# Two gated attention layers with mixtures of experts on one core: the first layer's experts computed for the chosen tokens only

## The chip, the cores and the metric

The kernel runs on one core of a Trainium2 chip, in float32 except where it splits numbers into bfloat16 parts. The metric is the device time of one execution in microseconds (us), the median of several. One execution of each kernel is also recorded by the hardware profiler. Engine names are those of the profile: PE is TensorE's matmuls, PEld its weight loads, DVE VectorE, ACT ScalarE, POOL GpSimd, SP SyncE, which issues most DMAs.

## The reference, cut to what matters

The input x is 16 batches of 256 tokens of width 256. Four units follow one another, each added to x with a gate tanh(g): unit 0, cross attention of 16 heads; unit 1, self attention plus a mixture of 8 linear experts; unit 2, attention over context and tokens; unit 3, causal attention, a second, larger mixture of experts, and norms. Unit 1 is what the change is about:

```python
    def _L0_ffn_ref(x, W_qkv, b_qkv, W_gate, b_gate, W_experts, b_experts):   # E = 8, TOP_K = 2, D = 256
        ...
        attn_out = jnp.einsum('bhqk,bkhd->bqhd', attn, v).reshape(B, S, D)
        gate = jax.nn.softmax(x @ W_gate + b_gate, axis=-1)
        top_g, top_i = jax.lax.top_k(gate, TOP_K)
        combine = jnp.sum(jax.nn.one_hot(top_i, E, dtype=x.dtype) * top_g[..., None], axis=2)
        expert_out = jnp.einsum('bsd,edf->bsef', x, W_experts) + b_experts
        moe_out = jnp.einsum('bsef,bse->bsf', expert_out, combine)
        return attn_out + moe_out
    ...
    x = x + jnp.tanh(g_xattn[0]) * _L0_xattn_ref(ctx_2048, _layernorm(x, axis=-1), L0_xattn_b, itok_Bx1_68_817)
    x = x + jnp.tanh(g_ffn[0]) * _L0_ffn_ref(_layernorm(x, axis=-1), L0_ffn_W_qkv, ...)
```

## The kernel before, in words

The kernel has two phases. The attention phase does all four units. Its work is cut into 64 jobs (u, b), a unit and a batch, unit by unit, and each job into steps: XT transposes the normalised rows; K, Q, V are projections; KSPLIT and QSPLIT (POOL, three operations each) split them into bfloat16 parts, which go through memory (STACK, ROWS) to become operands; S are scores whose row maxima DVE takes; M (POOL, five small operations) and MT bring the maxima in place; T are the scores again, of which ACT takes the exponentials; PV is the product with the values; OT turns the result back, and FIN adds it to x. Each token tile has 128 rows, so a batch has two.

Which engine does which step when is not left to the hardware. A planner (`orders`) plays the steps at build time with a cost per step (`STAGES`) and writes down one fixed order for each engine (`ORDER`), looking at most eight jobs ahead. Each engine then works down its list and waits on semaphores. A step that waits holds up all that stands behind it on its engine. Small rings of buffers tie jobs to each other: the transposed rows `xt` have three buffers, so XT of a job waits until the third job before it has used its own; `o` has three, `xs` seven, and the steps in `PRE` (XT, K, Q, V and all that makes expert results) share two PSUM banks.

In unit 1 each job also has the mixture. GATE computes logits, GEXP and six TOP steps (DVE) the two best experts and a weight for all eight, with zeros for six. MBIAS starts the sum with the weighted biases, and 8 EXPERT steps per job (two experts each, both halves of the inner dimension) compute all eight experts for all tokens, of which DVE adds each with its weight:

```python
                    elif name == "EXPERT":
                        t, e = k
                        end_pre(step, pe.matmul(bank[:, :], xt_now[:, turn, t * P:(t + 1) * P], wexp[:, turn, e:e + 2, :].rearrange("p e n -> p (e n)"),
                                                start=turn == 0, stop=ends), ends)
```

The second phase, the expert phase, does unit 3's large mixture in another way: `route` sorts all tokens by expert into 71 slot tiles of 128 rows (64 full ones and one more for each of seven experts), and `run_experts` fetches the rows of a tile with an indirect DMA, computes one expert for them, and stores the results with another. `combine` adds them. This phase is not touched.

## Time and profile before

| | us |
|---|---|
| median of three runs | 2621.05 (2614.16 to 2621.49) |
| the profiled execution, its own time | 2617.61 |
| its span, first to last instruction | 2615.9 |
| unit 0, to its last FIN | 361.6 |
| unit 1, from there to its last FIN | 617 |
| unit 2, from there to 1566 | 587 |
| unit 3, to 1902 | 336 |
| sorting, expert phase and combine | 714 |

Times below are read on the profiled execution, from the start of its span. The stage borders are starts of the last step of a unit; the stages overlap by some tens of us, as the first steps of a unit begin during the one before it.

### The profile page before, as it was taken

Reading aid. Unit: us, or ns where it says so; the run is one execution under the profiler, and the core shown is the slowest. Engines: PE = TensorE matmul, PEld = TensorE weight load, DVE = VectorE, ACT = ScalarE, POOL = GpSimd, SP = SyncE. Lnnn points to the kernel's source line nnn. Section 1 sums busy time; section 2 is a strip of 40 time slices with the busy share of each in tenths; the row PEclk is TensorE's granted clock in tenths of the full one; section 3 lists DMA queues with packets and bytes.
Section 4 is the critical chain, followed back from the end, with each engine's and each line's share of the span. In section 5 each row is a group of like instructions: output and inputs, shape, how many; then the busy total and the mean of one; then the engine's idle time right before and its main releaser. Section 6 shows DMA issues by size and latency. Waiting matters only on the chain. (4 is left out here: it accounts for less than half of the span.)

```text
span 2615.9 us, 52259 instructions
## 1 busy us (share of the span) xinstructions
PE 2282.1 (87%) x17492; PEld 1575.9 (60%) x17493; DVE 1686.8 (64%) x4481; ACT 1362.3 (52%) x2398; POOL 978.5 (37%) x1850
## 2 busy tenths in 40 slices
PE   2889999899999999999999999899848999999910
PEld 1445555555455556666666666666538999999910
DVE  4878886676767666777767668767563444443458
ACT  3889863454336346777777777767601222222211
POOL 5555412213122225333322247878602333333321
PEclk7999998999899999999999999999958999999965
DMA  7878623315134245544455445555180111111144
GB/s 216 206 192 208 148 67 82 88 38 122 30 88 95 65 99 135 116 116 113 112 118 120 107 116 109 122 133 129 42 277 27 34 36 37 36 36 32 35 173 156
DMA packets 209839, 275.49 MB, mean 105 GB/s; under 512 B 32606, under 2 KB 156489, under 8 KB 203370
## 3 DMA queue, kind: packets, MB, share of 16 engines
q1 hardware_dynamic: 196074, 242.38, 37.3%
q0 software_dynamic: 6912, 17.97, 2.2%
q10 hardware_dynamic: 6656, 12.58, 1.3%
q8 instruction: 116, 1.90, 0.3%
q14 instruction: 81, 0.66, 0.1%
HBM read 193.12 MB, written 80.64 MB: 105 GB/s over the span
## 5 line engine op out<-in xcount | busy, mean ns | idle before, releaser
L1035 ACT ACTIVATE ex<-t_ps 128x512 f32<-128x512 f32 (+1 forms) x1280 | 685.7, 579 | 203.0 <-PE t_ps L941 157.9
L1183 DVE TENSOR_REDUCE mx<-s_ps 128x2 f32<-128x512 f32 (+1 forms) x1024 | 659.9, 683 | 197.2 <-PE s_ps L912 125.2
L941 PE MATMUL t_ps<-qs,ks 123*128 123x256 bf16 x2048 | 355.5, 277 | 8.7 <-ACT ex L1035 3.7
L964 PE MATMUL pv_ps<-ex,va 128*17 128x256 f32 (+1 forms) x5120 | 318.1, 374 | 1.3 <-POOL ex L1087 1.3
L1029 ACT ACTIVATE qs<-tr_ps 27x2048 bf16<-27x2048 bf16 x128 | 239.2, 1869 | 108.3 <-PE tr_ps L925 105.5
L882 PE MATMUL pre_ps<-wexp,xt 128*128 128x512 f32 x512 | 270.5, 634 | 3.1 <-DVE moe L1242 2.2
L941 PEld LDWEIGHTS t_ps<-qs,ks 123*128 123x128 bf16 x2048 | 176.9, 98 | 156.1 <-ACT ex L1035 68.2
L1582 PEld LDWEIGHTS x_up_ps<-x_rows_t,x_wnow 128*128 128x128 f32 x2272 | 266.4, 193 | 5.3 <-issue 0.9
L1582 PE MATMUL x_up_ps<-x_rows_t,x_wnow 128*128 128x128 f32 x2272 | 267.0, 276 | 1.1 <-DVE x_pre L1645 0.7
L1592 PE MATMUL x_y_ps<-wdn,x_act 128*128 x1136 | 257.1, 379 | 0.7 <-DVE x_y L1653 0.7
L1612 ACT ACTIVATE x_rows_t<-x_rt_ps 128x256 f32<-128x256 f32 x72 | 27.6, 383 | 436.7 <-PE x_rt_ps L1571 436.7
L1592 PEld LDWEIGHTS x_y_ps<-wdn,x_act 128*128 128x128 f32 x1136 | 210.3, 190 | 26.8 <-issue 1.1
L1095 POOL TENSOR_SCALAR mp<-mx 128x16 bf16<-128x16 f32 x128 | 34.3, 268 | 512.2 <-DVE mx L1183 492.9
L918 PE MATMUL s_ps<-ks,qs 99*128 99x256 bf16 (+1 forms) x1024 | 186.6, 284 | 36.2 <-DVE mx L1183 24.7
L964 PEld LDWEIGHTS pv_ps<-ex,va 128*17 128x17 f32 x5120 | 124.8, 97 | 139.3 <-issue 49.9
L1176 DVE CUSTOM_DVE_ANT_0 s_ps<-s_ps,late 128x128 f32<-128x128 f32 (+1 forms) x512 | 166.8, 388 | 45.4 <-PE s_ps L915 45.2
L912 PE MATMUL s_ps<-ks,qs 96*128 96x256 bf16 x1024 | 180.0, 274 | 15.0 <-DVE mx L1183 8.5
L1640 DVE COPY x_wnow<-wup 128x1024 f32 x144 | 98.9, 688 | 144.9 <-issue 82.9
L1242 DVE SCALAR_TENSOR_TENSOR moe<-pre_ps,comb,moe 128x256 f32<-128x256 f32 x256 | 123.4, 482 | 91.2 <-PE pre_ps L882 84.3
L1039 ACT ACTIVATE ot<-pv_ps 128x256 f32<-128x256 f32 x256 | 99.8, 390 | 133.2 <-PE pv_ps L964 130.8
L918 PEld LDWEIGHTS s_ps<-ks,qs 99*128 99x128 bf16 (+1 forms) x1024 | 86.4, 100 | 126.6 <-DVE mx L1183 73.3
L1078 POOL TENSOR_TENSOR ak<-ak,pk 128x512 f32<-128x512 f32 x64 | 74.7, 1167 | 218.8 <-ACT pk L1016 112.5
(248 smaller groups left out, 3739.7 us busy)
## 6 DMA issues: line engine op xcount, KB each, us to landing
q_parts<-pq SPq DMA_DIRECT2D x128, 192.0 KB
qs<-q_parts SPq DMA_DIRECT2D x64, 384.0 KB, 4.9
qs<-q_parts SPq DMA_DIRECT2D x192, 128.0 KB, 5.8
k_parts<-pk SPq DMA_DIRECT2D x96, 192.0 KB
ks<-k_parts SPq DMA_DIRECT2D x96, 192.0 KB
ks<-k_parts SPq DMA_DIRECT2D x288, 64.0 KB
ks<-ctx_k_parts SPq DMA_DIRECT2D x64, 192.0 KB
ks<-ctx_k_parts SPq DMA_DIRECT2D x192, 64.0 KB
```

The lines of the kernel that those rows point to most:

```text
L882: end_pre(step, pe.matmul(bank[:, :], xt_now[:, turn, t * P:(t + 1) * P], wexp[:, turn, e:e + 2, :].rearrange("p e n -> p (e n)"), start=t ...
L912: last = pe.matmul(dst[:, r * T:(r + 1) * T], q(src), key(r)[0:rows, h, :], start=True, stop=True)
L918: last = pe.matmul(dst[:, t * T:(t + 1) * T], q(t), key(0)[0:rows, h, :], start=True, stop=True)
L941: last = pe.matmul(dst[:, t * T:(t + 1) * T], key[0:ROWS, h, t * P:(t + 1) * P], qs[q_at][0:ROWS, h, :], start=True, stop=True)
L964: last = pe.matmul(pv_ps[i * VS:i * VS + VW, q0:T], val[:, t, k * QH + i, :], e, start=r == 0 and t == 0, stop=r == srcs - 1 and t == NT - ...
L1029: act.activation(qs[q_at][PRODUCTS:ROWS, k * HG:(k + 1) * HG, :], tr_b[PRODUCTS:ROWS, 0:T].unsqueeze(1).broadcast_to([ROWS - PRODUCTS, HG, ...
L1035: act.activation(ex[:, n % EXPS, 0:w], t_ps[n % 2][:, 0:w], ACT.Exp).then_inc(t_read, 1)
L1176: last = dve.tensor_tensor_reduce(out=seen, in0=seen, in1=late[:, 2 * P - w:2 * P], scale=1.0, scalar=FUTURE, op0=ALU.add, op1=ALU.max, ac ...
L1183: dve.tensor_reduce(dst, s_ps[n % S_BANKS][:, :].rearrange("p (a b) -> p a b", a=dst.shape[-1]), AX.X, ALU.max).then_inc(s_read, 1)
L1242: last = dve.scalar_tensor_tensor(out=moe[r][:, t, :], in0=bank[:, n * D:(n + 1) * D], scalar=comb[r][:, t, e + n:e + n + 1], in1=moe[r][: ...
L1582: last = pe.matmul(up_ps[h][:, g * P:(g + 1) * P], wnow[k][h][:, c, g * P:(g + 1) * P], rows_t[:, c, :], start=c == 0, stop=c == DC - 1)
L1592: last = pe.matmul(y_ps[:, 0:D], act_t[k][h][:, g, :], wdn[:, bass.ds(x, 1), f, :].rearrange("p e n -> p (e n)"), start=f == 0, stop=f == ...
```

## The change

The mixture of unit 1 is taken out of its jobs and done by slots, as the expert phase does the larger one.

- Unit 0 gains, after FIN of each batch: HNS, HNP, HNX (moments and normalised rows of the new x, DVE and POOL), STOREN (the rows to memory, SP), HT (transposed, PE and ACT) and HG (the gate's logits, PE and DVE). Unit 1 loads the rows (LOADN) and no longer computes them. HT writes the `xt` buffer of its job, and XT of unit 1 waits until HG of three jobs before has read it.
- When all 16 batches have their logits, a chain of 23 RC steps on DVE (some 75 instructions, each of which waits for the one before it), with RX, RANK and NAME on ACT, PE and POOL, sorts the tokens into 71 tiles. It is the computation of `route`, and it runs beside the first jobs of unit 1.
- Each of the 71 tiles has XR (POOL: indirect DMA of 128 rows into one of six buffers), XTT (PE fetches the number of the tile's expert into a register, then two transposes; ACT copies), XE (PE: the bias as a product of a one-hot with the three bfloat16 parts of the biases, then two products of 256 columns; DVE copies to one of four buffers) and XS (POOL: indirect DMA to memory). The planner counts them to jobs 2 to 7 of unit 1.
- GATE, GEXP, TOP, CT, MBIAS, EXPERT and FIN's addition of the mixture are gone. Unit 2 gains LOADY (512 KB of expert rows) and MOE (DVE, four additions) per job, ahead of its moments.
- Unit 3's weights `w1` and `wo` move into the memory of the spent experts and are loaded in unit 2. In the first block of the program the biases are loaded three times behind the expert weights, and DVE makes their parts, before it turns `w1x`.

```diff
+HOTS = 4
+NER, NY = 6, 4
+CHAIN = 23
+def tile_job(n):
+    return 1, 2 + n // 12
...
-    "GATE": [("pe", 0.9), ("dve", 0.65)], "GEXP": [("act", 0.22)], "TOP": [("dve", 0.6)],
-    "CT": [("pe", 0.25), ("act", 0.36)], "MBIAS": [("pe", 1.1), ("dve", 0.69)], "EXPERT": [("pe", 0.87), ("pe", 0.87), ("dve", 0.97)],
+    "XR": [("pool", 1.25), ("wire", 4.5)], "XTT": [("pe", 0.55), ("act", 0.39)], "XE": [("pe", 1.0), ("dve", 0.42)], "XS": [("pool", 1.25), ("wire", 4.5)],
...
-    free = [past(n, NQ, 0, (1, 2, 3)) for n in ("K", "Q", "V")] + [past("EXPERT", NQ, (t, e), (1,)) for t in range(NT) for e in range(0, E, 2)]
+    free = [past(n, NQ, 0, (1, 2, 3)) for n in ("K", "Q", "V")] + [past("HG", NQ, 0, (0,))]
...
+    for n in range(SLOT_TILES):
+        add(of("XR", n), rc(CHAIN - 1), of("XTT", n - NER))
+        add(of("XTT", n), of("XR", n), of("XE", n - 2))
+        add(of("XE", n), of("XTT", n), of("XS", n - NY))
+        add(of("XS", n), of("XE", n))
...
-                sp.dma_start(bexp[:, :], a["b0_exp"]).then_inc(small_loaded, 16)
...
-                sp.dma_start(w1[:, :, :], chunked(a["w1_qkv"])).then_inc(w_loaded, 16)
-                sp.dma_start(wo[:, :, :], chunked(a["w1_o"])).then_inc(w_loaded, 16)
+                for n in range(3):
+                    sp.dma_start(bexp[n * E:(n + 1) * E, :], a["b0_exp"]).then_inc(small_loaded, 16)
...
+                    elif name == "XTT":
+                        if k == 0:
+                            pe.wait_ge(tables_ready, 1)
+                        chosen[k] = pe.value_load(expert_of[0:1, k:k + 1], min_val=0, max_val=E - 1)
+                        begin_pre(step)
+                        pe.wait_ge(er_loaded[k % NER], 16 * (k // NER + 1))
+                        for c in range(DC):
+                            last = pe.transpose(bank[:, c * P:(c + 1) * P], er[k % NER][:, c * P:(c + 1) * P], ident[:, :])
                         end_pre(step, last)
-                    elif name == "EXPERT":
-                        t, e = k
-                        end_pre(step, pe.matmul(bank[:, :], xt_now[:, turn, t * P:(t + 1) * P], wexp[:, turn, e:e + 2, :].rearrange("p e n -> p (e n)"),
-                                                start=turn == 0, stop=ends), ends)
+                    elif name == "XE":
+                        wait_copied(pe, ("XTT", u, b, k))
+                        x = chosen.pop(k)
+                        pe.matmul(bank[:, 0:D], tile_is[:, k:k + 1].broadcast_to([3 * E, P]), bexp_parts[:, :], start=True, stop=False)
+                        for c in range(DC):
+                            last = pe.matmul(bank[:, 0:D], ert[k % 2][:, c, :], wexp[:, c, bass.ds(x, 1), :].rearrange("p e n -> p (e n)"),
+                                             start=False, stop=c == DC - 1)
+                        end_pre(step, last)
...
+                    elif name == "XR":
+                        if k == 0:
+                            pool.wait_ge(tables_ready, 1)
...
+                        if k >= NER:
+                            wait_turned(pool, ("XTT", *tile_job(k - NER), k - NER))
+                        pool.indirect_dma_start(er[k % NER], None, n1_d.rearrange("b p t n -> (b p t) n"),
+                                                bass.IndirectOffsetOnAxis(ap=row_of[:, k:k + 1].bitcast(U32), axis=0)).then_inc(er_loaded[k % NER], 16)
+                    elif name == "XS":
+                        wait_copied(pool, ("XE", u, b, k))
+                        pool.indirect_dma_start(y1_d.rearrange("b p t n -> (b p t) n"), bass.IndirectOffsetOnAxis(ap=dest_of[:, k:k + 1], axis=0),
+                                                ey[k % NY], None, bounds_check=ROWS_OUT - 1, oob_is_err=False).then_inc(y_stored[k % NY], 16)
...
+                    elif name == "MOE":
                         dve.wait_ge(x_loaded[x_at], 16 * (nth_x + 1))
+                        dve.wait_ge(y_loaded[b % 2], 16 * (b // 2 + 1))
+                        for m in range(TOPK):
+                            for t in range(NT):
+                                last = dve.scalar_tensor_tensor(out=xs[x_at][:, t, :], in0=yb[b % 2][:, t * TOPK + m, :], scalar=first_share[:, b * NT + t, m:m + 1],
+                                                                in1=xs[x_at][:, t, :], op0=ALU.mult, op1=ALU.add)
```

How the change moves instructions, at three places. The first is PE where the first projection of unit 1 stands (`pre_ps<-xt,w`). `s_ps` are scores, `t_ps` the scores again; 16 heads of a batch make 32 matmuls of each. Before:

```order
L821 MATMUL pre_ps<-ident,xn 128x128 x4
L918 MATMUL s_ps<-ks,qs 128x256 x2
L975 MATMUL tr_ps<-ident,ot 128x128 x2
L918 MATMUL s_ps<-ks,qs 128x256 x2
L941 MATMUL t_ps<-qs,ks 128x256 x2
L918 MATMUL s_ps<-ks,qs 128x256 x2
L941 MATMUL t_ps<-qs,ks 128x256 x2
L975 MATMUL tr_ps<-ident,ot 128x128 x2
L964 MATMUL pv_ps<-ex,va 17x256 x8
L941 MATMUL t_ps<-qs,ks 128x256 x4
L925 MATMUL tr_ps<-ident_b,mp 27x128 x2
L918 MATMUL s_ps<-ks,qs 128x256 x4
L826 MATMUL pre_ps<-xt,w 128x256 x2
```

After; `ident,o` is HT, `wg,xt` is HG and `ident,xn` is XT of the first job of unit 1:

```order
L968 MATMUL pre_ps<-ident,o 128x128 x4
L1091 MATMUL tr_ps<-ident_b,mp 27x128 x2
L1130 MATMUL pv_ps<-ex,va 17x256 x8
L980 MATMUL pre_ps<-wg,xt 128x8 x4
L1084 MATMUL s_ps<-ks,qs 128x256 x4
L968 MATMUL pre_ps<-ident,xn 128x128 x4
L1107 MATMUL t_ps<-qs,ks 128x256 x4
L1141 MATMUL tr_ps<-ident,ot 128x128 x2
L1084 MATMUL s_ps<-ks,qs 128x256 x4
L973 MATMUL pre_ps<-xt,w 128x256 x2
```

Before, 384 of unit 0's 512 `t_ps` matmuls stand ahead of this projection; now 468 do, with 56 of the 64 matmuls of HG.

The second place is PE in the middle of the expert tiles. Before, between attention steps, one EXPERT turn (`pre_ps<-wexp,xt`) at a time:

```order
L918 MATMUL s_ps<-ks,qs 128x256 x4
L941 MATMUL t_ps<-qs,ks 128x256 x2
L882 MATMUL pre_ps<-wexp,xt 128x512
L941 MATMUL t_ps<-qs,ks 128x256 x4
L918 MATMUL s_ps<-ks,qs 128x256 x4
L882 MATMUL pre_ps<-wexp,xt 128x512
L941 MATMUL t_ps<-qs,ks 128x256 x4
L964 MATMUL pv_ps<-ex,va 17x256 x8
```

After (`ident,work` are the transposes of XTT, the ISA rows handle the register):

```order
L1043 MATMUL pre_ps<-bexp_parts,tile_is 128x256
L1045 ISA
L1045 MATMUL pre_ps<-wexp,work 128x256
L1045 ISA
L1045 MATMUL pre_ps<-wexp,work 128x256
L1043 MATMUL pre_ps<-bexp_parts,tile_is 128x256
L1045 ISA
L1045 MATMUL pre_ps<-wexp,work 128x256
L1045 ISA
L1045 MATMUL pre_ps<-wexp,work 128x256
L1034 TENSOR_LOAD first_expert_of
L1034 ISA x2
L1038 MATMUL pre_ps<-ident,work 128x128 x2
L1107 MATMUL t_ps<-qs,ks 128x256 x2
```

From the first fetch of an expert's number to the last expert product PE has 71 tiles and 178 `t_ps` matmuls, the attention of 5.6 jobs; 78 matmuls (2.4 jobs) of unit 1 stand ahead of it, and 8 jobs behind it.

The third place is POOL in the same stretch (`work<-normed` is XR, `first_expert_rows<-work` is XS, `ak`, `pk` are KSPLIT, `aq`, `pq` QSPLIT):

```order
L1237 DMA first_expert_rows<-work,first_dest_of 8192x256
L1233 DMA work<-normed,first_row_of 128x256 x3
L1262 TENSOR_TENSOR ak<-ak,pk 128x512
L1264 CAST pk<-ak 128x2x256
L1266 TENSOR_TENSOR pk<-ak,pk 128x2x256
L1262 TENSOR_TENSOR aq<-aq,pq 128x512
L1264 CAST pq<-aq 128x2x256
L1266 TENSOR_TENSOR pq<-aq,pq 128x2x256
L1237 DMA first_expert_rows<-work,first_dest_of 8192x256 x4
L1233 DMA work<-normed,first_row_of 128x256 x4
L1237 DMA first_expert_rows<-work,first_dest_of 8192x256 x2
L1233 DMA work<-normed,first_row_of 128x256 x2
```

Before, POOL had in unit 1 only such splits, the five operations of M and two for the moments of a job. Now 142 indirect DMAs stand there, with 12 M and 8 splits between the first and the last of them.

## Rows read from the trace of the kernel before

**Rows 1.** The page: busy time, share of the span and instructions of each engine.

```profile
PE 2282.1 (87%) x17492; PEld 1575.9 (60%) x17493; DVE 1686.8 (64%) x4481; ACT 1362.3 (52%) x2398; POOL 978.5 (37%) x1850
```

**Rows 2.** Windows by stage: length, busy time (instructions) of PE PEld DVE ACT POOL, PEclk, DMA share, GB/s.

```profile
31.00:361.60 330.60, 281.61 (x2495) 157.71 (x2496) 256.88 (x578) 258.81 (x439) 174.61 (x329) 0.94 0.75 180
361.60:978.70 617.10, 578.35 (x3333) 318.62 (x3332) 424.31 (x1040) 281.07 (x512) 143.94 (x282) 0.95 0.31 76
978.70:1566.00 587.30, 567.72 (x5142) 368.09 (x5140) 414.34 (x899) 441.40 (x757) 200.44 (x370) 0.99 0.50 116
1902.00:1971.00 69.00, 30.14 (x133) 28.74 (x133) 43.47 (x108) 0.42 (x1) 1.16 (x6) 0.50 0.81 259
```

**Rows 3.** FIN: its source line up to 362.4, and in the whole trace.

```profile
L1263 DVE SCALAR_TENSOR_TENSOR xs<-o,tanh_g,xs x16: 751/752/1427, 97.1 to 361.6; 128x512 f32<-128x512 f32 x16
...
L1263 DVE SCALAR_TENSOR_TENSOR xs<-o,tanh_g,xs x32: 750/752/1530, 97.1 to 978.7; 128x512 f32<-128x512 f32 x32
```

**Rows 4.** Groups of the whole trace: what the change removes.

```profile
L882 PE MATMUL pre_ps<-wexp,xt 128*128 128x512 f32 x512 | 270.5, 634 | 3.1 <-DVE moe L1242 2.2 <-DVE va L1167 0.8
...
L1242 DVE SCALAR_TENSOR_TENSOR moe<-pre_ps,comb,moe 128x256 f32<-128x256 f32 x256 | 123.4, 482 | 91.2 <-PE pre_ps L882 84.3
...
L878 PE MATMUL pre_ps<-bexp,combt 8*128 8x256 f32 x64 | 20.8, 450 | 10.8 <-DVE va L1167 10.3 <-DVE moe L1242 0.5
```

**Rows 5.** Windows of 5 us in unit 1, columns as in rows 2.

```profile
420.00:425.00 5.00, 0.90 (x5) 0.23 (x3) 4.90 (x11) 0.57 (x2) 4.64 (x6) 0.90 0.92 223
425.00:430.00 5.00, 4.86 (x14) 3.51 (x15) 2.28 (x10) 0.22 (x1) 1.65 (x3) 0.50 0.92 186
430.00:435.00 5.00, 5.00 (x8) 1.81 (x6) 2.06 (x11) 0.00 (x0) 0.00 (x0) 0.57 0.58 170
```

**Rows 6.** Timeline of the first block: start, us, engine, line, [idle before].

```profile
7.11 1.09 SPq L592 DMA_DIRECT2D wexp<-in_L_ffn_W_experts  x2
...
13.72 0.17 DVE L655 TENSOR_SCALAR bqk<-bqk 128x2 f32<-128x2 f32 x1
...
22.87 0.85 DVE L662 COPY wproj<-s_ps 128x256 f32<-128x256 f32 x2 [0.36 <-PE s_ps L683]
```

**Rows 7.** Window of 150 us within unit 0, columns as in rows 2.

```profile
150.00:300.00 150.00, 136.67 (x1288) 75.58 (x1290) 124.15 (x270) 131.64 (x222) 78.89 (x156) 0.99 0.79 185
```

**Rows 8.** Groups of the whole trace: nearest to what is added.

```profile
L826 PE MATMUL pre_ps<-xt,w 128*128 128x256 f32 x512 | 130.0, 383 | 2.8 <-ACT xt L998 1.7 <-DVE moe L1242 0.9
...
L1571 PE MATMUL x_rt_ps<-ident,x_rows 128*128 128x128 f32 x144 | 27.9, 275 | 8.4 <-DMA x_rows<-h_normed,x_row_now 8.4
...
L1149 DVE BATCH_NORM_STATS2 hstats<-o 128x6 f32<-128x256 f32 x32 | 12.0, 418 | 0.5
...
L1159 DVE TENSOR_SCALAR o<-o,hmv,hrstd 128x256 f32<-128x256 f32 x32 | 14.0, 479 | 1.9 <-POOL hrstd L1059 1.9
```

**Rows 9.** Groups of the whole trace: POOL's indirect DMAs and one part of a split.

```profile
L1535 POOL DMA_INDIRECT x_rows<-h_normed,x_row_now x73 | 73.1, 1001 | 62.3 <-POOL x_row_now L1533 58.9 <-DVE x_y L1653 3.5
...
L1543 POOL DMA_INDIRECT expert_rows<-x_y,x_dest_now x71 | 79.9, 1125 | 65.4 <-POOL x_dest_now L1541 65.4
...
L1078 POOL TENSOR_TENSOR ak<-ak,pk 128x512 f32<-128x512 f32 x64 | 74.7, 1167 | 218.8 <-ACT pk L1016 112.5 <-ACT pk L1014 91.7 <-ACT pk L1006 14.6
```

**Rows 10.** Timeline in the expert phase.

```profile
2210.13 1.25 POOL L1543 DMA_INDIRECT expert_rows<-x_y,x_dest_now  x1 [0.92 <-POOL x_dest_now L1541]
2210.56 0.69 DVE L1640 COPY x_wnow<-wup 128x1024 f32 x1 [1.78 <-PE x_up_ps L1582]
...
2217.38 1.00 POOL L1543 DMA_INDIRECT expert_rows<-x_y,x_dest_now  x1 [0.92 <-POOL x_dest_now L1541]
2218.33 0.69 DVE L1640 COPY x_wnow<-wup 128x1024 f32 x1 [2.31 <-issue]
```

**Rows 11.** Source line of PE's fetch in the expert phase: ns min/median/max.

```profile
L1564 PEldq TENSOR_LOAD <-expert_of x71: 298/312/498, 1980.8 to 2488.1; - x71
```

**Rows 12.** Source line L1535, the gathers of the expert phase, from issue to landing.

```profile
DMA to landing us min/median/max: 2.7/2.8/4.1
```

476 lines of the change are left out of this document (345 added, 131 removed).

## The prediction

> **What bounds the kernel now.** I began with the page's totals: PE is busy for 87% of the span [rows 1], but that is a mean over stages, so the windows by stage came next [rows 2]. They say which engine sets the pace of each. In unit 1, where the change works, PE is busy 578 of 617 us (94%), DVE 69%, ACT 46%, POOL 23%, the DMA engines 31%: a stage bound by PE. Unit 2 is so still more (568 of 587 us). Unit 0 is another matter. FIN of its 16 batches starts between 97.1 and 361.6 [rows 3], a pitch of 17.6 us, and a window in its middle shows PE at 91%, ACT 88%, DVE 83% and DMA 79% [rows 7]: four resources close together.
>
> The costliest groups then say what PE's time in unit 1 is: the dense experts are 270.5 us of PE and the weighted additions 123.4 us of DVE [rows 4]. Their sizes, 512 records in 256 matmuls of 512 columns, make 1.06 us a matmul. Last, windows of 5 us show how the stage runs: at 420 PE stands for 4 us while DVE and POOL are full, and the next 10 us have a granted clock of 0.50 and 0.57, the lower level (1.2 GHz) or mostly so [rows 5]: 4 us idle and 5 lost to the clock. The clock of the whole stage is 0.95 [rows 2], 31 us of 617 at most, which six such stalls would explain.
>
> **The change, step by step.** The profiled execution took 2617.6 us for a span of 2615.9, 3.4 us under the median of the runs; the sum is made on it. First the pieces that are added or removed in unit 1.
>
> - PE, removed: 270.5 + 20.8 (MBIAS) [rows 4], and 16 pairs of small transposes at 0.39 [rows 8], 6: 297 us.
> - PE, added: a 256-column float32 matmul costs 130.0 us over 256 (512 records), 0.51 us; the two transposes of a tile 27.9 over 72, 0.39 us [rows 8]. The one-hot product (24 rows, bfloat16) is in no row; it lies between nothing and a float32 one of the same width, 0.51; I take 0.25. A tile is 0.39 + 2 x 0.51 + 0.25 = 1.66 us, 71 tiles 118 us. NAME adds at most the 30 us of PE in the sorting stage, at a clock of 0.50 [rows 2]; 15 at full clock.
> - DVE, removed 123 us and the TOP steps; added 71 copies of some 0.4 us, and the chain, priced by the sorting stage that does the same: 43.5 us busy [rows 2].
> - POOL, added: 71 gathers of 1.00 us and 71 stores of 1.13, 151 us [rows 9].
>
> What is left to an attention job of unit 1? About 5% of its expert matmuls start ahead of the stage's border, so I give the window 95% of the unit, 15.1 jobs. PE: the mixture is 297 us, and GATE with 64 products of 8 columns at most 18 at the 0.28 of the smallest matmuls in rows 8; 95% of 315 is 299, and 578 - 299 = 279 us are 18.5 a job. ACT: 281 over 15.1, 18.6 us [rows 2]. So once the experts are away a job has two engines at 18.6 us, and by unit 0's ratio (a pitch of 17.6 with a busiest engine of 0.91 x 17.6 = 16.1 [rows 3, 7]) its pitch is 20.3.
>
> Now the terms.
>
> *First block, +6.* DVE now passes its wait for the small loads at once (13.72), and ends its last copy at 23.7 [rows 6]. The new loads stand behind 2 MB of experts issued at 7.1; at the 180 GB/s of rows 2's first window these need 12 us, so DVE goes on at 19, then has some twelve dependent operations of 0.2 to 0.4 us more, and turns `w1x` after them. Between nothing and 12.
>
> *Unit 0, +24.* Per job DVE gets two moments of 0.42, two normalisations of 0.48 [rows 8] and three smaller operations, some 2.3 us; ACT a copy no longer than FIN's 0.75 [rows 3]; PE four transposes, 0.78, and four small products, at most 1.1; DMA 256 KB, 1.4 us at 180 GB/s. DVE goes from 14.6 to 16.9 us per job, PE from 16.1 to as much as 18.0, ACT from 15.5 to 16.2, DMA from 13.9 to 15.3: PE may just pass the pitch of 17.6, and the others stand near 90% or above, in one fixed order with waits between them. Floor nothing, ceiling 16 x 2.3 = 37; I take 1.5 us a job.
>
> *Unit 1, 617 to 510, -107.* Three stretches, split where the order on PE has the first and the last fetch.
> (a) From unit 0's last FIN to the first gather: 5 us until the last logits are there, then the chain's 43.5 us on DVE together with 2.4 jobs of attention at 14.6 us of DVE (35 us): 83 us. DVE is the bound. The order also shows that XT of unit 1's first job now stands behind HG, 84 `t_ps` matmuls (2.6 jobs) later than before; these 2.4 jobs, less than DVE could do beside the chain otherwise, are that price.
> (b) Expert tiles: PE 118 + 5.6 x 18.5 = 222 us. POOL 151 + about 45 (12 M and 8 splits, five jobs of its 144/15.1 = 9.5 us [rows 2]) = 196. PE is the bound by a little; with two engines this close I take 230.
> (c) Eight jobs at 20.3, 163, and 10 until the splits that stood behind the last indirect DMAs have become operands: 173.
> Sum 486. The fetch of a tile's expert takes PE's sequencer 0.31 us [rows 11], 22 us in all if none lies behind queued matmuls. One step of lead before XE hides the use, not the fetch; in the expert phase it stands behind a long queue of matmuls, here between short ones. I take half, 11, and with what handles the register 12. And 12 for stalls with a low clock behind them, where before six of the kind shown [rows 5] cost some 9 each.
>
> *Unit 2, +8.* MOE is four additions of 0.48 [rows 4], 31 us on a DVE that is idle for 173 of 587 us under a PE at 97% [rows 2]. It is hidden unless it stands ahead of row maxima that PE waits for; floor nothing, ceiling 31. LOADY (4 MB in all) has a DMA at 50%, and the weights' 1 MB too: nothing. Unit 3 and the rest: nothing.
>
> 6 + 24 - 107 + 8 = **-69 us**: 2548.6 on the profiled execution, 2552 as a median.
>
> **A rule that speaks against it.** A store in the expert phase took 1.25 us when a DVE copy within SBUF began inside it, and 1.00 us when the copy came only at its end [rows 10]. The Trainium skill says why ("Advanced Engine Details and Errata", VectorE Performance Modes, Mode Summary): VectorE's second port to SBUF is shared with GpSimd, and two-port operations and GpSimd block each other. The trace agrees, with 0.25 us. Were all 142 transfers hit, POOL's 196 us would be 231 beside PE's 222: some 5 us of the sum, and DVE mostly reads PSUM in this stretch.
>
> **Rivals.**
>
> 1. *POOL becomes the bound: the idle time ahead of an indirect DMA is its own.* Every one in the trace stands 0.8 to 0.9 us behind the small copy before it, though that copy was done; 58.9 + 65.4 us for 143 of them [rows 9, 10], counted as idle. The group of a split shows idle time only for ACT's sake [rows 9], not behind POOL's own operations. If the instruction holds POOL for it, a DMA costs 1.9 us, POOL in (b) has 196 + 124 = 320 us, and M and the splits of the attention jobs wait in the same queue. Against it: the gap may be sequencer time that runs under the operation before, which no row shows, as none stands back to back. (b) becomes 320 for 230, +90; PE's fetches then lie in its idle time, -12. 2548.6 + 78 is 2627, 2630 as a median; if 0.15 us of each gap is only the wait for the copy, 2609. It is the one that can end slower: it decides from 0.5 us more per DMA (69 over 142), and (c)'s splits, which stand behind the last stores, can take it to 2645.
> 2. *The in-order stalls stay.* Unit 1 loses now some 55 us in six of them. If the new order, in which gathers, one-hots and attention meet on four engines, keeps 40 more than I counted, 2590. For it: stretches (a) and (b) have two near-bounds each. Against: the tiles are spread between attention steps, and there is less of them.
> 3. *It goes as the engines' sums allow.* Unit 0 hides its additions (+5), no fetch and no stall is seen: 2552 less 19, 12, 12 and 8, about 2500.
> 4. *The gathers come late.* They land in 2.8 us, 4.1 at most [rows 12], and six buffers give a lead of over 10 us at one tile per 3.2 us: not a rival worth a share, nor are four result buffers.
>
> **Chances.** Forecast (2525 to 2578) 0.36; POOL bound (2600 to 2645) 0.34; stalls (2578 to 2600) 0.17; full gain (2495 to 2525) 0.10; 0.03 for a slower case that I don't see. A measurement of this kernel can't tell about 0.3%, 8 us, from no change. Of rival 1's 0.34 I put 0.05 below 2613, 0.09 within 8 us of 2621 and 0.20 above. So faster 0.36 + 0.17 + 0.10 + 0.05 = 0.68, same 0.09, slower 0.23. The range for 8 in 10 runs from 2515 to 2637; the forecast's own is 2525 to 2578.
>
> **What would show it.** Right: unit 1 from its border to its last FIN in about 510 us; unit 0's last FIN at 392; the first gather 80 to 85 us behind that; PE above 90% between the first and last gather, POOL at 85% there; pitch of the last jobs about 20 us. Rival 1: the stretch of gathers over 290 us, PE under 75% in it, ACT and PE waiting for POOL's M and splits, and a gap ahead of each indirect DMA even where two follow each other. Rival 2: windows at a clock near 0.5 inside unit 1. Fetch cost: idle time of PE ahead of the transposes of `work` that ends for no other engine. A pitch in unit 2 well over 36.7 us (587 over 16) would show MOE in front of the maxima. The largest lever is the cost of one indirect DMA on POOL; the next, what unit 0's four nearly full resources do with 2.3 us more of DVE.

## The result, and the profile after

The changed kernel takes 2601.1 us (median of 10 runs, 2595.2 to 2607.3), the kernel before 2616.8 (10 runs, 2612.4 to 2621.5): ratio 0.9937, 95% interval 0.9925 to 0.995. It is faster, by 16 us (0.6%, clear of the noise) where 65 to 69 were forecast. That lies outside the forecast's own range and inside the one for 8 in 10, at the edge of the bracket that was given to rival 1; as the last part shows, rival 1 is not what happened, so the wide range held it by luck. The profiled execution took 2602.1 us for a span of 2600.3. One execution among all those below, of run e13, took 4650 us; no row here has a cause for it, and it stands in no number of this text.

The page's first rows (columns as in [rows 1]), then the windows by stage with borders as in [rows 2]: unit 0, unit 1, within it the stretch of the expert tiles, and unit 2. Here and in every run that stretch goes from the start of the first gather to the start of the last store (the last gather starts some 20 us earlier, at 723.4 here); the expectations below call it the stretch "from the first to the last gather".

```profile
PE 2188.8 (84%) x17577; PEld 1572.9 (60%) x17578; DVE 1615.6 (62%) x4177; ACT 1387.4 (53%) x2454; POOL 1145.2 (44%) x2015
```

```profile
31.00:400.85 369.85, 298.27 (x2613) 173.79 (x2613) 259.86 (x602) 268.35 (x450) 182.92 (x345) 0.96 0.70 172
400.85:940.49 539.64, 471.60 (x3395) 306.51 (x3395) 320.61 (x675) 305.41 (x571) 314.85 (x449) 0.95 0.57 144
494.11:746.27 252.16, 224.21 (x1434) 138.76 (x1432) 105.05 (x220) 121.60 (x239) 178.52 (x226) 0.97 0.46 125
940.49:1549.18 608.69, 562.26 (x5044) 359.28 (x5043) 440.94 (x923) 432.51 (x741) 184.29 (x349) 0.97 0.49 115
```

FIN's source line, of unit 0 and of the whole trace, answers to [rows 3]:

```profile
L1538 DVE SCALAR_TENSOR_TENSOR xs<-o,tanh_g,xs x16: 750/752/1252, 102.3 to 400.9; 128x512 f32<-128x512 f32 x16
L1538 DVE SCALAR_TENSOR_TENSOR xs<-o,tanh_g,xs x32: 750/752/1252, 102.3 to 940.5; 128x512 f32<-128x512 f32 x32
```

So by stage, against [rows 2, 3]: first FIN 102.3 for 97.1 (+5); from it to unit 0's last FIN 298.5 for 264.5 (+34); unit 1 539.6 for 617.1 (-77.5); unit 2, to its last PROJ, 608.7 for 587.0 (+22); the rest +1. The sum is -16. The borders hide work that moved across them. At the end of unit 1, two groups of PE between the last store and the last FIN of unit 1, and the same of the whole of unit 1 before, are the first projections of unit 2:

```profile
L973 PE MATMUL pre_ps<-xt,w1x 128*128 128x256 f32 x64 | 16.5, 383 | 0.0
L980 PE MATMUL pre_ps<-w1x,xt 128*128 128x256 f32 x13 | 3.5, 379 | 0.0
```

```profile
L826 PE MATMUL pre_ps<-xt,w1x 128*128 128x256 f32 x16 | 4.3, 392 | 0.5 <-ACT pk L1016 0.5
L833 PE MATMUL pre_ps<-w1x,xt 128*128 128x256 f32 x8 | 2.2, 392 | 0.0
```

With the 36 products of the first maxima (6.4 us, before 4 with 0.6), 26 us of PE work of unit 2 now lie in unit 1, 7 before. Measured in the same work, then, unit 1 won about 97 us and unit 2 lost about 41. PROJ, the last step of a job of unit 2, says the same; its source line before and after:

```profile
L1251 DVE SCALAR_TENSOR_TENSOR xs<-pre_ps,tanh_g,xs x16: 750/751/752, 1042.2 to 1565.7; 128x512 f32<-128x512 f32 x16
```

```profile
L1531 DVE SCALAR_TENSOR_TENSOR xs<-pre_ps,tanh_g,xs x16: 749/751/752, 984.2 to 1549.2; 128x512 f32<-128x512 f32 x16
```

The first PROJ comes 43.7 us behind the border where it came 63.5 behind it (20 us of work done earlier), the next nine have a pitch of 38.8 us for 34.3 (41 us lost), and the last six take 215 us in both. At the border of units 0 and 1 work moved the other way: before, 17 us of PE's mixture work and 26 of unit 1's score records ran ahead of unit 0's last FIN; now 4 such records do, and of the mixture only the new HG. So unit 0 takes 34 us more although those 17 us of PE's work have left it. Unit 2 is where most of the forecast went: 33 of the 53 us by which the sum of the terms is off, with about 10 each in units 0 and 1.

What happens there is one picture, which comes nine times with the same numbers. DVE and PE, timeline of one job of unit 2, and windows of 5 us around it:

```profile
1154.30 3.94 DVE L1434 SCALAR_TENSOR_TENSOR xs<-work,first_share,xs 128x256 f32<-128x256 f32 x4
1158.34 0.75 DVE L1451 BATCH_NORM_STATS2 stats<-xs 128x6 f32<-128x256 f32 x2
1159.12 0.25 DVE L1454 BATCH_NORM_AGGREGATE mv<-stats 128x2 f32<-128x6 f32 x2
...
1159.71 1.28 DVE L1514 TENSOR_REDUCE mx<-s_ps 128x1 f32<-128x512 f32 x2
```

```profile
1160.44 0.61 PE L1078 MATMUL s_ps<-ks,qs 96*128 96x256 bf16 x2 [2.23 <-DVE mx L1514]
```

```profile
1155.00:1160.00 5.00, 2.92 (x32) 1.39 (x20) 4.79 (x10) 3.52 (x7) 4.56 (x6) 1.00 0.46 102
1160.00:1165.00 5.00, 4.56 (x43) 2.12 (x44) 3.01 (x6) 1.68 (x3) 1.70 (x2) 0.66 0.33 88
```

Four additions stand in DVE's order as one block of 3.94 us with the moments behind it, 5 us in which no maximum is taken; PE runs dry for 2.2 us, and then its granted clock is 0.66 for the next window. The picture holds for the nine blocks from 998 on: each takes 3.93 us and is followed by a wait of 2.2 us, and after eight of the nine the granted clock falls to 0.50, the lower level (1.2 GHz). Of the seven blocks before them, five of which stand in unit 1, three bring a wait (1.3 to 2.8 us). MOE's source line and POOL's queue in the same microseconds say why the block is 3.94 long and not the four times 0.48 of the forecast:

```profile
L1434 DVE SCALAR_TENSOR_TENSOR xs<-work,first_share,xs x64: 472/824/1452, 836.3 to 1311.1; 128x256 f32<-128x256 f32 x64
```

```profile
1152.77 1.16 POOL L1262 TENSOR_TENSOR ak<-ak,pk 128x512 f32<-128x512 f32 x1 [6.28 <-ACT pk L1182]
1153.99 0.61 POOL L1264 CAST pk<-ak 128x512 bf16<-128x512 f32 x1
1154.68 1.22 POOL L1266 TENSOR_TENSOR pk<-ak,pk 128x512 bf16<-128x512 f32 x1
1155.86 1.34 POOL L1262 TENSOR_TENSOR aq<-aq,pq 128x512 f32<-128x512 f32 x1
```

```profile
945.45 1.79 DVE L1434 SCALAR_TENSOR_TENSOR xs<-work,first_share,xs 128x256 f32<-128x256 f32 x4
```

The planner put MOE exactly beside the splits of K and Q. The last line is a block with nothing of POOL beside it: 1.79 us, 0.48 an addition. Beside the splits the four take 0.58, 1.38, 1.27 and 0.83 us (985 ns on average), and POOL's subtraction 1.34 us for 1.16. I had priced MOE by a group that reads one operand from PSUM [rows 4]; MOE reads both from SBUF. The Trainium skill had the rule ("Advanced Engine Details and Errata", Miscellaneous Facts, GPSIMD Details): POOL shares a read and a write interface with DVE and conflicts with instructions that have two SBUF inputs. The trace agrees: in the same kernel the same four additions take 1.79 us without POOL and 3.93 beside its splits.

### The profile page after: what moved, and what is told of

It reads as the page before. It is cut to its first block and busy times, and to the rows that moved or that the text cites. A ratio compares the mean times of both kernels' runs of the same rounds, so it can differ in the third digit from the quotient of the medians.

```text
span 2600.3 us, 53021 instructions
## 1 busy us (share of the span) xinstructions
PE 2188.8 (84%) x17577; PEld 1572.9 (60%) x17578; DVE 1615.6 (62%) x4177; ACT 1387.4 (53%) x2454; POOL 1145.2 (44%) x2015
## 5 line engine op out<-in xcount | busy, mean ns | idle before, releaser
L1107 PE MATMUL t_ps<-qs,ks 123*128 123x256 bf16 x2048 | 363.6, 283 | 21.2 <-ACT ex L1201 9.4
L1130 PE MATMUL pv_ps<-ex,va 128*17 128x256 f32 (+1 forms) x5120 | 329.8, 386 | 1.5 <-POOL ex L1271 1.0
L1078 PEld LDWEIGHTS s_ps<-ks,qs 96*128 96x128 bf16 x1024 | 86.4, 98 | 96.0 <-DVE mx L1514 75.8
L1928 DVE TENSOR_TENSOR x_y<-x_y_ps,bdn 128x256 f32<-128x256 f32 x71 | 30.1, 424 | 160.8 <-PE x_y_ps L1867 156.7
```

The costliest lines, as they stand in the source:

```text
L1078: last = pe.matmul(dst[:, r * T:(r + 1) * T], q(src), key(r)[0:rows, h, :], start=True, stop=True)
L1107: last = pe.matmul(dst[:, t * T:(t + 1) * T], key[0:ROWS, h, t * P:(t + 1) * P], qs[q_at][0:ROWS, h, :], start=True, stop=True)
L1130: last = pe.matmul(pv_ps[i * VS:i * VS + VW, q0:T], val[:, t, k * QH + i, :], e, start=r == 0 and t == 0, stop=r == srcs - 1 and t == NT - ...
```

## The experiments

Each run's ratio is to the kernel before on the same chip. Windows quoted from them have the columns of [rows 2]; where a run's work differs from the reference its expectation says how. Runs e1 to e4 shared a chip, e5 to e8 a second, e9 to e16 a third, e17 and e18 a fourth.

**MOE, its work and its place.** e1 cuts the width of the additions, e2 makes four steps of the one:

```
-  last = dve.scalar_tensor_tensor(out=xs[x_at][:, t, :], in0=yb[b % 2][:, t * TOPK + m, :], ...
+  last = dve.scalar_tensor_tensor(out=xs[x_at][:, t, 0:8], in0=yb[b % 2][:, t * TOPK + m, 0:8], ...
```

> The changed kernel, with each of the four MOE additions of a job of unit 2 cut from 256 columns to 8 (the slots' results are no longer added to the other 248 columns); all steps, loads and waits stand where they were. Theory A (four additions in one block on DVE, 3.9 us, stand ahead of row maxima that PE waits for, and PE's clock falls behind that): the pitch of unit 2's first ten jobs falls from 38.7 to about 34.5 us, unit 2 from 609 to about 588 us, the median to about 2580. Rival B (the 256 KB more of LOADY per job, or the planned order itself, slows unit 2): pitch stays 38 us or more, unit 2 above 603, median about 2599.

```
-  "MOE": [("dve", 1.95)]
+  "MOE": [("dve", 0.98)]
-            x = add("MOE", 0, x, y)
+            for n in range(NT * TOPK):
+                x = add("MOE", n, x, y)
```

> The changed kernel with the whole computation, MOE split into four steps of one addition each (0.98 us in the planner's table), so that maxima may stand between them. Theory A (block): PE's waits for maxima in unit 2 fall from 29.5 to about 12 us, unit 2 takes 590 to 600 us, median about 2587. Rival B: the work itself, 33 us more on DVE, is what costs, wherever it stands: unit 2 stays at 605 to 610, median 2600.

Measured: e1 2581.1 us, ratio 0.9844 (0.9826 to 0.9863); e2 2557.1 us, 0.9748 (0.9732 to 0.9764). The split, with all the work, beats the cut. Unit 2 takes 596 us in e1 (pitch of the first ten PROJs 37.4), 573 in e2 (34.9), 609 in the changed kernel (38.8) and 587 before (34.3). e1's median is what theory A gave, but its pitch is nearer rival B: 13 us came in unit 2, and 12 in unit 1, for which A had nothing. MOE's line in e2, in the e1 run the windows of 2 us around the block, and in e2 those of 5 us at the same place of a job:

```profile
L1437 DVE SCALAR_TENSOR_TENSOR xs<-work,first_share,xs x64: 471/479/1391, 834.6 to 1275.4; 128x256 f32<-128x256 f32 x64
```

```profile
1136.00:1138.00 2.00, 0.83 (x6) 0.52 (x7) 1.93 (x7) 1.20 (x3) 1.76 (x3) 1.00 0.52 141
1138.00:1140.00 2.00, 1.75 (x16) 0.73 (x17) 1.98 (x5) 1.59 (x3) 0.34 (x1) 0.68 0.47 111
1140.00:1142.00 2.00, 2.00 (x28) 0.74 (x20) 0.00 (x0) 0.10 (x1) 1.27 (x1) 0.50 0.46 134
```

```profile
1132.00:1137.00 5.00, 4.91 (x55) 2.19 (x53) 4.86 (x11) 3.62 (x7) 3.99 (x4) 1.00 0.27 69
1137.00:1142.00 5.00, 4.24 (x50) 2.40 (x50) 4.54 (x12) 3.55 (x7) 2.25 (x8) 1.00 0.61 158
```

In e1 the block still stands in one piece, and it is still 2.7 us long:

```profile
1132.66 2.69 DVE L1434 SCALAR_TENSOR_TENSOR xs<-work,first_share,xs 128x8 f32<-128x8 f32 x4
885.47 0.76 DVE L1434 SCALAR_TENSOR_TENSOR xs<-work,first_share,xs 128x8 f32<-128x8 f32 x4
```

The second line is a block with nothing of POOL beside it. Beside the splits two of the four small additions take 1.1 and 1.2 us for 8 columns: so most of that time goes with POOL and not with the columns, and cutting the width shortened the block by a third only. PE is busy 0.83 of 2 us, and its clock falls to the lower level (0.50, 1.2 GHz) behind that. In e2 the additions of unit 2's jobs stand mostly as two and two or three and one, with row maxima between them. Some still take 1.4 us beside the splits, but no wait of PE for the maxima is over 0.8 us, and unit 2's mean clock is 1.00. The waits for maxima that PE's weight loads see in unit 2, changed kernel, then e2:

```profile
PEld s_ps L1078 <- DVE mx L1514: 73.8, 135, 2.5
```

```profile
PEld s_ps L1079 <- DVE mx L1509: 50.3, 143, 0.8
```

Before it was 54.3 us with a longest of 0.8. So theory A holds in its place, and my number for it (590 to 600) was too high: 36 us, more than twice the 13 that removing the width gives. In the same work e2's unit 2 is still 5 us longer than before the change (573 + 19 against 587). A new order came with the split, which e1 kept as it was; the two runs together, and the waits, are what speaks for the block. What costs is the length of the one block that PE must outlast, first as a wait and then as clock.

**The fetch of the expert.**

```
-  chosen[k] = pe.value_load(expert_of[0:1, k:k + 1], min_val=0, max_val=E - 1)
+  chosen[k] = k % E
```

> The changed kernel, but PE takes expert n mod 8 for tile n as a constant instead of fetching the number from the table (so tiles get the wrong weights); no fetch and no register work is left on PE. Theory A (fetch and register work are paid in full on PE's path): 0.3 for the fetch and 0.2 for the registers, 71 times, so the stretch from the first to the last gather falls from 253 to about 220 us, unit 1 from 540 to 505, median about 2566. Rival B (they lie under queued matmuls): the stretch stays within 5 us of 253. The prediction's 12 us would be between: 241, median 2589.

2599.9 us, 0.9921 (0.9904 to 0.9937). The stretch of the tiles:

```profile
491.25:737.19 245.94, 223.09 (x1434) 139.26 (x1432) 105.50 (x221) 120.58 (x239) 178.97 (x225) 0.97 0.46 127
```

252 became 246, and the changed kernel itself, run again (e10, below), had 249. The fetch (306 ns, with 151 of register work) costs at most these 6 us of 32 (71 times 0.46): close to rival B, though 2 us outside its bound of 5. My 12 was at least twice too much.

**The indirect DMAs on POOL.** e4 moves both kinds of transfer to SP as plain DMAs, on the changed kernel; e13, e14 and e15 do it with the stores, the gathers and both on e2. The planner's price goes from `("pool", 1.25)` to `("sp", 0.5)`, and it makes a new order.

```
-  pool.indirect_dma_start(er[k % NER], None, n1_d..., bass.IndirectOffsetOnAxis(ap=row_of[:, k:k + 1]...
+  sp.dma_start(er[k % NER], n1_d...[k % TILES * P:(k % TILES + 1) * P, :])
```

> The changed kernel, but a tile's rows are read and written as 128 consecutive rows by plain DMAs of SP, issued where the planner puts them at 0.5 us of SP, so the slots hold the wrong rows; POOL has no indirect DMA in unit 1. Theory A (142 indirect DMAs of about 1.3 us on POOL hold up M and the splits, and slow DVE): the stretch from the first to the last gather falls from 253 to about 230 us and what follows it from 193 to about 175, unit 1 from 540 to about 500, median about 2560. Rival B (PE sets the stretch): unit 1 stays within 8 us of 540, median 2595 or more.

> MOE split; a tile's results are written as 128 consecutive rows by plain DMAs of SP (so they lie in the wrong rows), the gathers stay indirect on POOL. Theory A (a store in POOL's queue waits for DVE's copy, 22 us in the stretch, and holds M and the splits behind it): most of the 20 to 27 us of e4, unit 1 at 508 to 515 us against 531. Rival B (POOL's load as such): half of it, as in e14, unit 1 at about 520. Rival C (the order that the planner makes): no gain.

> MOE split; a tile's rows are read as 128 consecutive rows by plain DMAs of SP (the wrong rows), the stores stay indirect on POOL. Theory A (stores hold the queue): little gain, unit 1 within 8 us of 531. Rival B (POOL's load as such): half of e15's gain, unit 1 at about 520.

> MOE split, gathers and stores both plain DMAs of SP (e4 on the split's base). Gain of e4 again, unit 1 at about 505 to 510 us against 531; if the gain of e4 was in how MOE's block met the rest, it is smaller, above 520.

e4 took 2568.6 us (0.9802, 0.9782 to 0.9821), e13 2561.8 (0.9781), e14 2568.7 (0.981), e15 2551.6 (0.9762, 0.9723 to 0.9801). Unit 1 in e4 and in e15:

```profile
399.47:912.32 512.85, 461.74 (x3382) 303.61 (x3383) 315.64 (x673) 302.54 (x569) 165.89 (x299) 0.96 0.59 153
```

```profile
395.32:906.14 510.82, 460.26 (x3384) 302.83 (x3385) 315.82 (x669) 302.79 (x569) 164.55 (x298) 0.96 0.61 154
```

Against 539.6 and 531.2 (e9, below) this is 27 and 20 us; e13 has 521.7 and e14 526.6, so 10 and 5 for one kind: rival B's number for the stores, within theory A's 8 us for the gathers. Neither alone gives most of it, so it is not the stores' wait for DVE's copy alone; the stores weigh more. The tile stretch itself falls to 231 us in e4 and 229 in e15, near theory A's 230, but in the new order it holds 108 fewer of PE's matmul records (17 us less busy in e15 than in e9), and what follows it takes 189 us for the 175 expected. DVE's busy time moves by 5 us and 2, so DVE held up by the transfers is not it either. That leaves M and the splits queued behind transfers, which is argued, not shown: the order changed too. Their medians are not to be compared, since in e13 to e15 the new order also made what lies behind unit 2 15 to 20 us longer.

**Unit 0's new work.** On e2, e5 narrows moments and normalisation to 8 columns, e6 keeps one of HT's four transposes and one of HG's four products, e16 does both.

```
-  s.done(dve.bn_stats(hstats[b % 2][:, t, :], src[:, t, :]))
+  s.done(dve.bn_stats(hstats[b % 2][:, t, :], src[:, t, 0:(D if u else 8)]))
   ...
```

> MOE split as before, and in unit 0 the new moments and normalisation (HNS, HNX) work on 8 columns instead of 256, so their results are wrong; every step, wait and DMA stands where it was. Theory A (unit 0's new term is DVE work that its order cannot hide): about 1.6 us of DVE a job less, unit 0's pitch falls from 19.8 to about 18.4 us and its last FIN comes 20 us or more earlier than 399. Rival B (it is the order and the waits between engines that the new steps bring, not their work): the last FIN comes within 8 us of 399.

> MOE split as before, and in unit 0 HT transposes one of four blocks and copies that block alone, and HG makes one of its four products (so the first layer's gate logits are wrong); every step and wait stands where it was. Theory A (PE's and ACT's part of the new work, some 1.3 us of PE and 0.4 of ACT a job, sets the pitch): the last FIN of unit 0 comes 15 us or more earlier than 399. Rival B (order and waits): within 8 us of 399. If both this and the run with small moments leave 399 as it is, the order holds the loss.

> MOE split; in unit 0 both cuts of e5 and e6: moments and normalisation over 8 columns, one of four transposes, copies and products of the gate (its logits are wrong); all steps, waits and DMAs stay. Theory A (the work explains unit 0, and its parts add): the last FIN at 399 less 5.5 and 13, about 380, which is 14 us of 34 left to order, waits and DMA. Rival B (the work explains all of it): 370 or less. Rival C (order and waits hold it): 385 or more, since with one part gone the other holds the pace.

The last FIN of unit 0 came at 393.5, 385.8 and 391.0. The three took 2585.3, 2581.2 and 2554.9 us, but the first two ran on a chip with a trouble of its own (next but one) that lies behind unit 0. By its bounds e5 is rival B; e6, 13 us earlier than 399, lies between its two. e16's window of unit 0 has a clock of 0.91, e6's 0.98, so the three don't rank:

```profile
31.00:391.01 360.01, 284.54 (x2473) 158.77 (x2473) 246.82 (x603) 263.34 (x450) 183.03 (x345) 0.91 0.70 176
```

From first to last FIN it is 293.5, 284.7 and 288.5 us against 298.5 in the changed kernel (294.9 in e2, 297.8 in e9) and 264.5 before. In e16 PE and DVE are busy 285 and 247 us, where they were 282 and 257 before [rows 2], and still 20 us or more of the 34 stay: rival C, order and waits, though e16's lower clock is part of what it shows and can't be taken out. The window of 150 us that answers to [rows 7] goes with that. PE, DVE and ACT are each less busy than before, and no engine is at its limit:

```profile
150.00:300.00 150.00, 128.79 (x1194) 73.80 (x1194) 119.06 (x283) 120.73 (x202) 84.98 (x162) 0.97 0.80 191
```

Which of the waits sets the pace I did not find; STOREN's DMA was not tried.

**The first block.** In the changed kernel DVE waits for the biases:

```profile
19.24 0.28 DVE L767 CAST bexp_parts<-bexp 24x256 bf16<-24x256 f32 x1 [4.49 <-DMA bexp<-in_L_ffn_b_experts]
...
27.00 0.85 DVE L790 COPY wproj<-s_ps 128x256 f32<-128x256 f32 x2 [0.35 <-PE s_ps L811]
```

e7 moves three lines, on e2:

```
   sp.dma_start(bproj[:, :], ...)
+  for n in range(3): sp.dma_start(bexp[n * E:(n + 1) * E, :], a["b0_exp"])
   sp.dma_start(wg0[:, :, :], ...)
   ... w0, wexp
-  for n in range(3): sp.dma_start(bexp[n * E:(n + 1) * E, :], a["b0_exp"])
```

> The whole computation, MOE split, and the three loads of the experts' biases issued ahead of the other weights instead of behind 2 MB of experts. Theory A (DVE's wait of 4.5 us for them in the first block is what the first block lost): DVE's last setup copy ends at about 23.5 instead of 27.9, the first FIN comes at 98 to 99 instead of 102 to 104, the median falls by 4 us against the split alone (2557), to about 2553. Rival B (the weights of the first products, now three loads later, or unit 0's own pace take it back): no change in the time of unit 0's last FIN (399).

First FIN at 97.3, as before the change, unit 0's last at 395.1 for 399. Theory A for the two FINs; its time, 2591.9 us (0.99, 0.9881 to 0.9918), is 35 us worse than e2's on another chip, and what follows shows where.

**A chip on which the tile stretch is longer.** e5, e6, e7 and e8 ran together on the second chip. In all of them the tile stretch took 274 to 289 us, though e5, e6 and e7 have e2's order there and DVE and POOL are as long busy. PE is busy 245 us in e7 for 226 in e9, with as many records and a mean clock of 0.90 for 0.96. e7's window, its waits of one kind, and one of them:

```profile
488.38:777.68 289.30, 244.59 (x1434) 146.82 (x1432) 105.83 (x220) 121.19 (x239) 178.71 (x225) 0.90 0.41 109
```

```profile
DVE work L1429 <- remote: 22.2, 7, 6.6
...
573.58 1.08 POOL L1238 DMA_INDIRECT first_expert_rows<-work,first_dest_of  x1 [0.15 <-issue]
...
582.28 1.13 PE L1046 MATMUL pre_ps<-wexp,work 128*128 x4
...
584.96 0.42 DVE L1429 COPY work<-pre_ps 128x256 f32<-128x256 f32 x1 [6.65 <-remote]
```

XE's copy waits for two things: PE's product and the store four tiles back. "remote" says only that the profile found nothing that ended the wait, and no profile of the other chips has such a wait. When I wrote the next four expectations I took it for a store that lands late. The semaphore events in the trace don't bear that out. The copy above starts when the semaphore of PE's product is raised, at 584.94; the store four tiles back, issued at 573.58, had all its 16 landing events by 578.4. All the waits marked "remote" in these four runs, ACT's for products of PE included, ended with a semaphore that PE raises: PE's products were done later (here 1.5 us) than the ends that the profile models for them. Of the landing events of the stores only about half are in these traces, so their times can't be compared with other chips. Why PE is slower there is open. Four more runs, on a third chip, asked whether the edits were at fault; e9 is e2 again, e10 the changed kernel again, e11 has six buffers of results in the same order, e12 both that and the biases first.

```
-  NER, NY = 6, 4
+  NER, NY = 6, 6
```

> The same kernel as e2 (MOE split into four steps), beside the others of this call on one chip. In e2 the stretch from the first to the last gather took 252 us; in the four kernels built on it that ran later (e5 to e7 with the same order there) 285 to 289 us, with DVE waiting up to 6.8 us for stores of a tile's results to land (a releaser 'remote' that the earlier profiles don't have). Theory A (the landing times differ from chip to chip or from day to day, and the kernel feels it): either 252 us again with no such waits, or 285 with them, the same for all kernels of this call. Rival B (the small edits of e5 to e7 cost 35 us there): 252 us here, whatever the others do; median 0.975 of before.

> The changed kernel itself, on the same chip as e9. If transfers land as in its first profile: 0.994 of before, stretch of gathers 252 us. If they land late: the stretch 285 us, and the ratio 1.005 or so. Either way e9 is 35 to 45 us faster (the split's worth), most of it in unit 2 (609 against 573 us).

> MOE split, and six buffers of a tile's results instead of four, with every instruction in the place where it stands with four (the planner still counts four). Theory A (DVE's wait for a store that frees a results buffer is what late landings cost): where e9 has waits on stores, they are gone or below 2 us, and the stretch of gathers falls to about 255 us; where e9 has none, no change. Rival B (late gathers, or something else, hold the stretch): within 5 us of e9 in any case.

> MOE split, six buffers of results, and the biases loaded first: the candidate for a version that beats both. Theory A (the first block's 4.5 us and the late stores are separate terms that add): 4 to 6 us faster than e11, about 0.973 of before. Rival B: unit 0's order takes the start back, within 2 us of e11.

e9 2557.7 (0.9779, 0.9742 to 0.9815), e10 2602.4 (0.9933, 0.9908 to 0.9958), e11 2556.1 (0.976), e12 2549.4 (0.9741, 0.9715 to 0.9767). The stretch is 249 to 252 us in all four, with no "remote" wait: the chip, or its state at that time, and not the edits. Whether six buffers would change anything on the second chip is not tested, and by what ended the waits there is no reason to expect it. The split's 45 us are there again (e9 and e10 on one chip); of the 38 by which their profiled executions differ, 35 lie in unit 2 (571.9 and 607.1 us) and 5 in unit 1. The biases give 6.7 (e11 and e12).

**How the tiles are spread.** e8 gives the planner the tile's price from the trace (0.8 and 1.5 us for PE, on e2); e17 and e18 change the job that a tile is planned with, on e12:

```
-    return 1, 2 + n // 12
+    return 1, 2 + n // 9        (e17; 18 in e18)
```

> The whole computation, MOE split, and the planner told what a tile takes on PE in the trace: 0.8 us for the two transposes with what stands before them (was 0.55) and 1.5 us for the bias and the two products (was 1.0). Theory A (the order of the tile stretch is planned for tiles 0.75 us shorter than they are, 53 us in all, so attention steps come late): from the first to the last gather about 240 instead of 252 us, and unit 1 some 12 us shorter than 533. Rival B (the order hardly depends on it; POOL's queue and PE's own work set the stretch): unit 1 within 5 us of 533.

> The whole computation on e12's base; the planner gives tile n to job 2 + n // 9 of unit 1 instead of 2 + n // 12, so 71 tiles stand beside eight jobs' attention, not six. Theory A (crowding on POOL and PE's order around each tile cost 22 us in the stretch, and thinner tiles let PE fill the gaps): unit 1 10 to 15 us under e12's 530, median about 2538. Rival B (the loss goes with each tile, wherever it stands): unit 1 within 5 us of 530, median 2547 to 2552.

> As e17, with job 2 + n // 18: four jobs' attention beside the tiles. Theory A: POOL, with 150 us of DMAs and some 60 of waits for DVE beside four jobs, becomes the bound of a stretch of about 230 us and attention piles up behind it: unit 1 10 us or more over 530. Rival B: within 5 us of 530.

e8 took 2608.4 us (0.9976, 0.996 to 0.9992) beside e7's 2591.9 on the same chip, which has the biases first, and unit 1 570 us for 569: honest prices bought nothing there. The tile stretch was 11 to 15 us shorter than in e5 to e7 and what follows it as much longer; all four ran on the chip with the longer stretch, and elsewhere e8 was not run. e17 2562.5 (0.981, 0.9777 to 0.9842), e18 2540.2 (0.9712, 0.9686 to 0.9737). Unit 1 took 530.1 us in e12, 525.9 in e17 and 513.5 in e18. The windows of the tile stretch and from there to the last FIN, e12 and e18:

```profile
487.86:736.45 248.59, 220.21 (x1434) 136.25 (x1432) 105.36 (x221) 121.68 (x239) 178.94 (x225) 0.99 0.46 126
736.45:924.47 188.02, 174.23 (x1437) 115.13 (x1438) 134.07 (x271) 143.55 (x260) 97.08 (x163) 0.98 0.77 189
```

```profile
489.87:722.65 232.78, 210.32 (x1245) 132.83 (x1244) 91.85 (x189) 103.29 (x206) 175.91 (x215) 0.95 0.47 127
722.65:910.03 187.38, 180.68 (x1609) 118.48 (x1608) 146.01 (x300) 159.04 (x287) 86.09 (x161) 1.00 0.74 186
```

My theory A had it the wrong way round: denser is better, POOL at 76% does not bind, and PE's idle time in the two windows falls from 42 to 29 us. Why thinner tiles also gain 4 us in unit 1 (its whole time is worse, since what lies behind unit 2 takes 16 us longer in its order) stays open. e18 is the best version found: it beats the kernel before by 2.9% and the changed one by about 2.3%. Its margin over e12, 0.9712 against 0.9741 on another chip, is within the two intervals; the 17 us in unit 1 are clearer.

## Why the prediction came out as it did

*Unit 2, +8: the step that failed.* It was priced as four additions of 0.48 that hide on an idle DVE, with the condition written beside it ("unless it stands ahead of row maxima that PE waits for") and a ceiling of 31. The condition was met by nine blocks of the sixteen in full, the additions took 0.82 (median) because POOL split beside them, and each of the nine brought a wait of 2.2 us, eight also a lower clock. In the same work it is +41, nine times 4.5 us of pitch, past my ceiling of 31, since that had the additions at 0.48 (all 64 took 56 us) and left out the clock. The split gives 36 of it back; the 5 that stay are what my +8 priced. The idle share of DVE, 173 of 587 us [rows 2], said nothing about whether 4 us in one piece fit.

*Unit 0, +24 against +34.* The additions themselves were no larger than thought; the pitch rose by 2.3 us, to 19.9, which is the ceiling of 37 nearly reached. I read four resources near their limit and took the middle, and I did not credit the 17 us of PE's mixture work that leave unit 0. e5, e6 and e16 say that at most some 14 us are the work; which wait makes the rest is open.

*Unit 1, -107 against -77.5, or -97 in the same work.* (a) 93 us against 83, DVE busy 78 of them: the bound was right, the DVE-bound stretch has its own waits. (b) PE busy 224 us against 222 worked out, but 252 us passed, 28 idle where I allowed 8 here and 24 more for fetch and stalls in the sum. The groups of that stretch:

```profile
L1045 PE MATMUL pre_ps<-wexp,work 128*128 x284 | 82.0, 412 | 0.0
L1237 POOL DMA_INDIRECT first_expert_rows<-work,first_dest_of x71 | 72.5, 1021 | 42.5 <-DVE work L1428 21.9 <-issue 19.4 <-ACT work L1192 1.2
L1233 POOL DMA_INDIRECT work<-normed,first_row_of x71 | 69.7, 982 | 26.4 <-issue 14.6 <-DVE first_row_of L1389 3.5 <-PE pre_ps L1038 3.1
L1038 PE MATMUL pre_ps<-ident,work 128*128 128x128 f32 x142 | 29.0, 287 | 10.9 <-issue 6.4 <-DVE work L1428 1.9 <-ACT pk L1180 0.7
L1043 PE MATMUL pre_ps<-bexp_parts,tile_is 24*128 24x256 bf16 x71 | 19.8, 279 | 5.3 <-ACT pq L1180 2.5 <-DVE va L1498 2.0 <-ACT work L1192 0.6
```

A tile costs PE 131 us over 71, 1.84 us for my 1.66; the one-hot bias 0.28 for the 0.25 chosen. That the sum held to 1% is luck: the tiles took 13 us more than my 118, and the attention between them 93 for my 104. (c) 194 us against 173: the last seven FINs of unit 1 have a pitch of 19.8 (20.3 forecast), and the excess is mostly the 19 us of unit 2's work. The fetch's 12 was at most 6.

*First block, +6 against +5.* Right, and e7 and e12 show the wait to be its cause.

*Rival 1, POOL bound (0.34), is refuted.* Where two indirect DMAs stand back to back and wait for nothing the gap is 0.30 us (median of 45 gathers and of 44 stores), not 0.9: so 0.5 us or more of each gap in [rows 9] went with the small copy before it. POOL is busy 71% of the stretch. Yet with the transfers off its queue unit 1 is some 20 to 27 us shorter (e4, e15), which neither the forecast nor the rival has: below the bound, and not free. *Rival 2, in-order stalls*, is nearest in kind to what came, but at 2601 it is outside its own bracket, and mostly in unit 2, not in the unit for which it was written. *Rival 4, late gathers*, had no share, and no run shows it. *The port rule* was right that DMAs would lose little (DVE's busy time moves by 2 to 5 us without them). It was weighed in the wrong unit, and its other half, two SBUF inputs, not at all.

## What to carry to other kernels

On an in-order engine price an added step by its longest piece against what the engine that waits for it has in hand, not by the engine's idle share: here blocks of 3.9 us under a PE at 97% cost 4.5 us of pitch each, and the same additions with other work between them cost 0.6. When an operation reads two SBUF operands on VectorE, look at what GpSimd does in the same microseconds. And when a change moves a stage's border, count a few instructions of the next stage on either side before dividing the blame. Before a wait is put down to a transfer, see which of its semaphores ended it.

## What the hardware showed that I had not expected

An all-SBUF VectorE addition of 128x256 took 0.48 us alone and 0.58 to 1.38 beside GpSimd's subtractions and casts; cut to 8 columns it took 0.22 us alone and up to 1.2 beside them. GpSimd's subtraction went from 1.16 to 1.34 us beside the wide additions. Indirect DMAs issue every 1.3 us when back to back (1.00 busy, 0.30 between). In e1 PE was busy 0.83 us of 2, and the next two windows of 2 us had a granted clock of 0.68 and 0.50. And on one chip of the four of the experiments the tile stretch took 285 to 289 us in an order that took 249 to 253 elsewhere, with as many matmul records of PE that were busy 239 to 245 us instead of 220 to 226, while the kernel before took 2616 us there and 2617 to 2621 on the others.
